# Counting out-degrees in the typed layer instead of beside the slot tables, and strewing GpSimd's marks among its fetches

## Chip, cores and metric

One core of one Trainium2 chip. The metric is the device time of one execution in microseconds (us), median of three runs. Shorter is better.

## What is computed

The reference is a graph network on 6250 nodes and 206250 edges (100000 random ones, the same turned round, and a self loop for each node, sorted by destination) with 128 features. Four layers follow each other, each added to its input and normalised:

```python
edge_index = jnp.stack([src, dst])
x = _layernorm(x + _L0_gnn_ref(x, ..., src, dst, edge_type_3, node_type_3), axis=-1)   # typed
x = _layernorm(x + _L1_gnn_ref(x, ..., edge_index, edge_weight), axis=-1)              # hyperbolic
x = _layernorm(x + _L2_gnn_ref(edge_index, x), axis=-1)                                # degree-normed
x = _layernorm(x + _L3_gnn_ref(x, edge_attr_64, src, dst, ...), axis=-1)               # edge features
```

Only the third layer needs the out-degree of every node, the number of edges with this source: `deg = segment_sum(ones, row)`, `norm = deg^-1/2[row] * deg^-1/2[col]`. The first, typed, layer sums a message of each edge, chosen by edge type and source type, into the edge's destination.

## The kernel before

All stages are blocks in which each engine runs its own queue; engines meet at semaphores, and at a barrier between blocks. The stages of this case, in order of time:

**Set-up (0 to 281 us).** Edges are loaded, their keys are made (`dbkt`, `dloc`: bucket of 128 nodes and place in it, of the destination; `sbkt`, `sloc`: the same of the source), and in-degrees are counted. The keys lie in `big`, the one large buffer, whose ranges are used again by the later stages. A count goes by batches of 16 columns (of 1612, so 101 batches): `hist_hot` makes on VectorE two one-hot tables in bf16, one of 128 places (L358, 128x2048) and one of 49 buckets (L359, 128x784), and `hist_sum` multiplies them on TensorE, 16 small matmuls (L366) into one PSUM tile. `hist_hot` of a batch waits for the matmuls of the batch two before it (`s_hist_mm`), since the tables are doubled.

**Slot tables (281 to 624 us, from L978).** 62 iterations (`GB`): 13 (`JB`) over slots that come from `chunk3`, a piece of the edge list loaded by four DMAs (L981, L982, `s_chunk`), and 49 (`NB`) over slots that GpSimd fetches, one indirect DMA of 128 x 4 KB for each (L1032, `s_took`, a ring of `GR` = 4). In iteration n VectorE and ScalarE pick keys (`pick`: L1087 to L1090, L1138, L1139), TensorE turns them (L1212), ScalarE stores them (L1145), VectorE splits the weight (L1099 to L1101) and SyncE writes the table out (L1001). In the same iterations the typed messages of a bucket of nodes are made: TensorE L1186, L1192, L1199, ScalarE L1150, L1156, L1163, L1164, SyncE's store L990. TensorE's `rows` (L1199) waits until ScalarE has emptied PSUM (L1164), and ScalarE's copy waits for TensorE.

GpSimd's queue in this stage is written out by hand: 49 indirect DMAs that put marks of 4 B into a table (L1016), one small gather (L1021), then the 49 fetches. Fetch b from the fifth on waits until slot table b + 9 has been picked. SyncE reads the marks back before table `MARK_LOAD` = 12 (L993), VectorE spreads them along the edges (`fill_forward`, before table `MARK_SCAN` = 20), and SyncE stores the result (L998, `edge_pairs`).

Out-degrees are counted here: `AHEAD` = 44 batches on VectorE and TensorE before the first pick, and the other 57 spread over the iterations (`outs(*shares[n])`), the last thing that an iteration does on TensorE.

**Adjacency blocks (624 to 2206 us)** use neither the keys nor the count.

**Typed layer (2206 to 3308 us, from L1558).** 456 groups of 512 edges. Of 24 groups (a turn) 13 come ready from DRAM by SyncE (L1564) and 11 are fetched by GpSimd, four indirect DMAs each (L1581, 836 in all), whose descriptors GpSimd prepares; I call that a preparation. SyncE brings their edge features (L1568). VectorE makes the one-hot table of a group (L1595, waits for TensorE's matmuls two groups back), adds the sums of the group two before it from PSUM to `acc` (L1620) and, in the first 17 turns, adds a step of the node's own row (L1612). TensorE does four matmuls a group (L1673) when table and features are there; PSUM banks 0 to 5 are a ring of Q = 6. A slot of the ring of QG = 8 fetched groups is free again when the matmuls eight groups back are done.

```python
pool.indirect_dma_start(out=got4[:, h, u, 0:D], out_offset=None, in_=typed_rows,
    in_offset=bass.IndirectOffsetOnAxis(ap=pairs4i[:, g, u, 0:1], axis=0)).then_inc(s_got[h], 16)
```

The pairs that this gather reads (`pairs4`) lie at the top of `big`. The functions that the change touches:

Of the kernel before, what the change touches and what calls it, by code (L numbers as in the profile page):

```python
# [147 lines left out]
def build(nc, x, src, dst, attr, etype, weight, ntype, w_e, b_e, w_n, b_n, w1, b1, w3, w3e, b3, out):  # L148
    ctx = ExitStack()
    with ctx:  # L150
# [90 lines left out]
        next_i = next_c.bitcast(I32)  # L241
        keys = []
        for _ in range(4):
            c, at = cut(at, CW // 2)
            keys.append(c.bitcast(BF16))
        dbkt, sbkt, dloc, sloc = keys
# [107 lines left out]
        def hist_hot(dve, lo, hi, n, c0, sl):  # L354
# [7 lines left out]
        def hist_sum(pe, to, n, sl, opens=False, closes=False):  # L362
# [405 lines left out]
        bias_sq = room(D)  # L768
        c1 = small[:, 11 * NB:11 * NB + 8]
# [200 lines left out]
        MARK_LOAD, MARK_SCAN = 12, 20  # L970
        AHEAD = 44
        shares = [(AHEAD + (HB - AHEAD) * n // GB, AHEAD + (HB - AHEAD) * (n + 1) // GB) for n in range(GB)]

        with nc.Block() as block:
# [36 lines left out]
            def _(pool):  # L1011
                pool.wait_ge(s_first, 1)
                beyond = pool.to_reg(MARKS - 1)
                for b in range(NB):
# [4 lines left out]
                pool.wait_ge(s_same, 1)  # L1019
                pool.sem_inc(s_turn, 1)  # L1020
                pool.indirect_dma_start(  # L1021
                    out=kind_i, out_offset=None, in_=ntype.rearrange("(n o) -> n o", o=1),
                    in_offset=bass.IndirectOffsetOnAxis(ap=head_i, axis=0)).then_inc(s_heads, 16)
                pool.iota(head_v, pattern=[[0, 1]], base=0, channel_multiplier=4 * CL,
                          allow_small_or_imprecise_dtypes=True).then_inc(s_pairs, 1)
                for b in range(NB):
                    n = JB + b
                    if b >= GR:
# [5 lines left out]
                        in_offset=bass.IndirectOffsetOnAxis(ap=first_i[:, b:b + 1], axis=0)).then_inc(s_took[b % GR], 16)  # L1034
                for k in range(GR):
# [3 lines left out]
            def _(dve):  # L1039
# [28 lines left out]
                def outs(j0, j1):  # L1068
                    for j in range(j0, j1):
                        hist_hot(dve, sloc, sbkt, HB + j, j * TT, (HB + j) % 2)  # L1070
                outs(0, AHEAD)
# [56 lines left out]
                dve.wait_ge(s_hist_mm, 2 * HB)  # L1128
                link(dve.tensor_copy(outdeg, out_count))
# [50 lines left out]
            def _(pe):  # L1180
                def outs(j0, j1):
                    for j in range(j0, j1):
                        hist_sum(pe, out_count, HB + j, (HB + j) % 2, opens=j == 0, closes=j == HB - 1)
# [19 lines left out]
                outs(0, AHEAD)  # L1203
                for n in range(GB):
# [13 lines left out]
                    outs(*shares[n])  # L1218
# [45 lines left out]
        pairs_at = big_words - NG * 2 * U  # L1264
        assert at <= pairs_at
        pairs4 = big[:, pairs_at:big_words].rearrange("p (g u r) -> p g u r", g=NG, u=U)
# [246 lines left out]
        xT4, at = cut(at, D)  # L1513
        assert at <= pairs_at
        OWN = 3
# [37 lines left out]
        with nc.Block() as block:  # L1553
# [33 lines left out]
            def _(dve):  # L1587
# [27 lines left out]
                def add(g, h, b, owned):  # L1615
# [22 lines left out]
                for r in range(LAG):  # L1638
                    add(NG - LAG + r, (NG - LAG + r) % Q, bucket[r], NB * OWN_STEPS)
# [12 lines left out]
            def _(pe):  # L1652
                pe.wait_ge(s_clear, 5)

                def turn(i, own_):
                    g0 = i * TURN
                    for pos in range(TURN):
                        h, k = pos % Q, pos % HS
# [11 lines left out]
                        slot_free(pe, s_acc, g0 + pos, Q)  # L1670
# [4 lines left out]
                        last.then_inc(s_mm, 1)  # L1675
                in_own_turns(pe, turn)
# [642 lines left out]
```

## Time and profile before

| | |
|---|---|
| median of 3 runs | 5259.34 us (5254.54 to 5260.63) |
| the profiled execution, its own time | 5261.47 us |
| its span, first to last instruction | 5259.7 us |
| mean granted TensorE clock | 0.934 |
| busy: PE, DVE, ACT, POOL | 72%, 62%, 23%, 43% |

PE is TensorE (PEld its weight loads), DVE VectorE, ACT ScalarE, POOL GpSimd, SP SyncE. A row of the timeline gives start and duration in us, engine, line, operation, output and input, and in brackets how long the engine had been idle and what ended that. "issue" is time in which an engine waited for nothing that the profile shows. The share of busy time is an average over stages with different limits, so each stage is read by itself.

### The profile page before, as it was taken

How to read it: one execution, taken by the hardware profiler on the slowest of the kernel's cores; microseconds unless marked ns; L12 is line 12 of the kernel's file. 1: busy time of each engine (PE TensorE's matmuls, PEld its weight loads, DVE VectorE, ACT ScalarE, POOL GpSimd, SP SyncE). 2: the span in 40 equal slices, each digit the busy share in tenths (PEclk: the TensorE clock that was granted, in tenths of full speed). 3: DMA queues.
4: the chain of work that ended last, by engine and by line, in shares of the span. 5: the costliest groups of instructions: out<-in, count | busy, mean ns of one | idle time of the engine just before them, and what ended most of it. 6: DMA issues, size and time to landing. Idle time of an engine off the chain costs nothing. (4 is left out here: it accounts for less than half of the span.)

```text
span 5259.7 us, 100150 instructions
## 1 busy us (share of the span) xinstructions
PE 3770.5 (72%) x38930; PEld 2751.6 (52%) x38930; DVE 3260.5 (62%) x4529; ACT 1204.4 (23%) x2110; POOL 2254.5 (43%) x2050
## 2 busy tenths in 40 slices
PE   4357755555555555377777676389999599989997
PEld 3345555555555555366666666345555244444444
DVE  7796898999999999455555554756666600230012
ACT  0025655555555555100000000400000200010000
POOL 0051378777777777577777777000000003000300
PEclk9998898999999999688998988699999799989998
DMA  9646797999999999865666656198888267656654
GB/s 315 212 115 238 236 343 276 327 346 340 336 338 340 343 344 330 222 165 166 171 165 165 169 162 158 22 332 305 301 305 304 91 203 227 198 165 202 217 187 142
DMA packets 695303, 1252.28 MB, mean 238 GB/s; under 512 B 366488, under 2 KB 511532, under 8 KB 685772
## 3 DMA queue, kind: packets, MB, share of 16 engines
q1 hardware_dynamic: 564028, 779.03, 46.1%
q10 hardware_dynamic: 60300, 314.88, 15.4%
q0 software_dynamic: 70576, 152.66, 11.4%
q8 instruction: 298, 4.88, 0.4%
q14 instruction: 101, 0.83, 0.0%
HBM read 792.49 MB, written 506.62 MB: 247 GB/s over the span
## 5 line engine op out<-in xcount | busy, mean ns | idle before, releaser
L1398 POOL DMA_INDIRECT big<-typed_msgs,big x988 | 1198.1, 1213 | 376.9 <-issue 307.8
L1446 PE MATMUL psum<-big 128*128 128x98 bf16 x7936 | 859.4, 208 | 649.8 <-DVE big L1428 629.4
L1446 PEld LDWEIGHTS psum<-big 128*128 128x128 bf16 x7936 | 766.0, 97 | 694.1 <-DVE big L1428 673.6
L2088 PE MATMUL psum<-big 128*128 128x512 bf16 (+1 forms) x4704 | 992.1, 373 | 82.6 <-DMA big<-adj 82.6
L1673 PE MATMUL psum<-big 128*128 128x192 f32 x3648 | 743.1, 364 | 307.8 <-DMA big<-typed_msgs,big 302.9
L1581 POOL DMA_INDIRECT big<-typed_msgs,big x836 | 830.8, 994 | 275.3 <-issue 244.8
L1673 PEld LDWEIGHTS psum<-big 128*128 128x128 f32 x3648 | 686.9, 215 | 371.8 <-issue 248.5
L1447 PE MATMUL psum<-big 128*128 128x49 bf16 x7936 | 845.5, 190 | 0.9 <-issue 0.9
L1448 PE MATMUL psum<-big 128*128 128x49 bf16 x7936 | 842.4, 186 | 2.7 <-issue 2.7
L1448 PEld LDWEIGHTS psum<-big 128*128 128x128 bf16 x7936 | 791.7, 100 | 3.1 <-issue 3.1
L2088 PEld LDWEIGHTS psum<-big 128*128 128x128 bf16 x4704 | 460.4, 98 | 605.9 <-DMA big<-adj 83.0
L1447 PEld LDWEIGHTS psum<-big 128*128 128x128 bf16 x7936 | 770.5, 97 | 11.1 <-issue 10.9
L1898 PE MATMUL psum<-big 128*128 128x416 f32 x1984 | 656.1, 494 | 63.4 <-DVE big L1932 62.4
L2135 POOL DMA_INDIRECT big<-spill,spill_row x98 | 92.7, 946 | 1420.0 <-DMA spill<-big 1390.7
L1428 DVE TENSOR_TENSOR big<-big 128x2400 bf16<-128x2400 bf16 x496 | 692.7, 1397 | 0.0
L1595 DVE SCALAR_TENSOR_TENSOR big<-iota,node,big 128x512 f32<-128x512 f32 x456 | 342.0, 750 | 517.4 <-PE psum L1673 502.5
L1425 DVE TENSOR_TENSOR big<-big 128x2048 bf16<-128x2048 bf16 x496 | 602.2, 1214 | 0.0
L1932 DVE STREAM_TRANSPOSE big<-big 128x3136 f32<-128x3136 f32 x124 | 427.2, 3445 | 239.6 <-PE psum L1898 221.2
L1486 ACT CAST big<-psum 128x784 bf16<-128x784 f32 x496 | 404.9, 816 | 675.7 <-PE psum L1448 574.7
L1898 PEld LDWEIGHTS psum<-big 128*128 128x128 f32 x1984 | 378.0, 191 | 341.1 <-issue 82.5
L1488 ACT COPY big<-psum 128x784 f32<-128x784 f32 x496 | 433.3, 874 | 0.0
L1423 DVE TENSOR_TENSOR big<-big 128x800 bf16<-128x800 bf16 x496 | 280.6, 566 | 68.9 <-POOLq L1402 50.1
(320 smaller groups left out, 2732.9 us busy)
## 6 DMA issues: line engine op xcount, KB each, us to landing
wadj<-big ACTq DMA_DIRECT2D x248, 784.0 KB
big<-wadj SPq DMA_DIRECT2D x124, 1568.0 KB, 7.3
big<-adj SPq DMA_DIRECT2D x210, 896.0 KB, 4.8
adj<-big ACTq DMA_DIRECT2D x62, 1568.0 KB
big<-staged SPq DMA_DIRECT2D x247, 384.0 KB, 3.3
staged<-big SPq DMA_DIRECT2D x61, 1536.0 KB
big<-edge_feats SPq DMA_DIRECT2D x456, 128.0 KB, 3.0
edge_feats<-in_edge_attr SPq DMA_DIRECT2D x1, 51562.5 KB, 163.3
```

Of the source, the lines that this page charges most:

```text
L1398: pool.indirect_dma_start(out=sgot4[:, c, u, 0:D], out_offset=None, in_=typed_rows, in_offset=bass.IndirectOffsetOnAxis(ap=pairs4i[:, g, u ...
L1425: dve.tensor_tensor(lo_b[:, q, :, :].rearrange("p t (c d) -> p t c d", d=2), in_twos(lo_ramp).to_broadcast([P, TT, P // 2, 2]), all_column ...
L1428: dve.tensor_tensor(hi_b[:, q, :, 1:4, :].rearrange("p t s (c d) -> p t s c d", d=2), hi.unsqueeze(2).to_broadcast([P, TT, 3, HC // 2, 2]) ...
L1446: pe.matmul(to[:, 0:2 * NB], lo, hi_b[:, q, t, 0:2, 0:NB], start=True, stop=False)
L1447: pe.matmul(to[:, NB:2 * NB], lo, hi_b[:, q, t, 2, 0:NB], start=False, stop=False)
L1448: last = pe.matmul(to[:, NB:2 * NB], lo, hi_b[:, q, t, 3, 0:NB], start=False, stop=True)
L1488: act.copy(wadj_st[:, k, b // 2, :, b % 2 * TT:(b % 2 + 1) * TT], made_in(b % 2)[:, :, NB:2 * NB].rearrange("p t s -> p s t")).then_inc(s_ ...
L1581: pool.indirect_dma_start(out=got4[:, h, u, 0:D], out_offset=None, in_=typed_rows, in_offset=bass.IndirectOffsetOnAxis(ap=pairs4i[:, g, u, ...
L1673: last = pe.matmul(ps[h][:, 0:ACCW], hot4[:, k, u, :], got4[:, pos % QG, u, :], start=(u == 0), stop=(u == U - 1))
L1898: last = pe.matmul(ps[c][:, 0:(b1 - b0) * 32], rows, turned[:, n % RT, q * QROW + b0 * 32:q * QROW + b1 * 32], start=(m == 0), stop=(m == ...
L1932: dve.transpose(turned[:, n % RT, :].rearrange("p (h i) -> p h i", i=32), wring[:, n % RW, :].rearrange("p (h g) -> p h g", g=32)).then_in ...
L2088: last = pe.matmul(ps[c % 2][:, 0:len(blocks) * P], terms_[:, k, b * D:(b + 1) * D], ring_a[:, m % RA, 0:len(blocks), s * P:(s + 1) * P], ...
```

## The change

The source keys `sbkt` and `sloc` move to the top of `big`, where they survive until the typed layer, and `pairs4` moves down below them. The 101 batches leave the slot tables; in the typed layer batch j is made on VectorE in group 4j + 1 and multiplied on TensorE after group 4j + 3, from tables of its own, and the count is copied out at the layer's end. Its PSUM tile lies in bank 5, so the ring of the group sums has 5 banks instead of 6. In GpSimd's queue the first four fetches come first, then the small gather, then three marks ahead of each further fetch; marks are read back before table 36 and spread before table 42.

```diff
-        MARK_LOAD, MARK_SCAN = 12, 20
-        AHEAD = 44
-        shares = [(AHEAD + (HB - AHEAD) * n // GB, AHEAD + (HB - AHEAD) * (n + 1) // GB) for n in range(GB)]
+        MARK_LOAD, MARK_SCAN = 36, 42
...
-                for b in range(NB):
+                def mark(b):
                     pool.sem_inc(s_turn, 1)
                     pool.indirect_dma_start(out=marks, ...).then_inc(s_marks, 16)
+                def fetch(b):
                     n = JB + b
                     if b >= GR:
                         pool.wait_ge(s_sb_st, n - GR + 1)
                         pool.wait_ge(s_slw_st, n - GR + 1)
                     ...
+                for b in range(GR):
+                    fetch(b)
+                pool.wait_ge(s_same, 1)
+                ...
+                marked_to = 0
+                for b in range(GR, NB):
+                    for m in range(marked_to, min(NB, marked_to + 3)):
+                        mark(m)
+                        marked_to = m + 1
+                    fetch(b)
...
-                outs(0, AHEAD)
                 dve.wait_ge(s_chunk, 16 * 4)
...
                         pick(n)
-                        outs(*shares[n])
...
-        pairs4 = big[:, pairs_at:big_words].rearrange("p (g u r) -> p g u r", g=NG, u=U)
+        pairs4 = big[:, pairs_at:kept_at].rearrange("p (g u r) -> p g u r", g=NG, u=U)
...
+        OUT_EVERY = NG // HB
+        PQ = 5
...
+                def out_hot(g):
+                    j, r = divmod(g, OUT_EVERY)
+                    if r == 1 and j < HB:
+                        hist_hot(dve, sloc, sbkt, HB + j, j * TT, (HB + j) % 2, out_lo, out_hi)
...
                         one_hot(i, pos)
                         ...
-                            add(g0 + (pos - LAG), (pos - LAG) % Q, bucket[pos % Q], owned)
+                            add(g0 + (pos - LAG), bucket[pos % Q], owned)
+                        out_hot(g0 + pos)
                         own(i, pos, own_)
...
+                dve.wait_ge(s_hist_mm, 2 * HB)
+                dve.tensor_copy(outdeg, out_count).then_inc(s_clear, 1)
+                dve.wait_ge(s_clear, 6)
...
-                        slot_free(pe, s_acc, g0 + pos, Q)
+                        slot_free(pe, s_acc, g0 + pos, PQ)
...
                         last.then_inc(s_mm, 1)
+                        c, r = divmod(g0 + pos, OUT_EVERY)
+                        if r == 3 and c < HB:
+                            hist_sum(pe, out_count, HB + c, (HB + c) % 2, opens=c == 0, closes=c == HB - 1, lo_hot=out_lo, hi_hot=out_hi)
```

GpSimd's queue in the slot tables before the change; 206336x1 is the table of marks, 128x1024 a fetch, 128x1 the small gather:

```order
L1016 DMA marks<-big 206336x1 x49
L1021 DMA big<-in_node_type,big 128x1
L1024 IOTA big 128x1
L1032 DMA big<-edge_fields,big 128x1024 x49
```

The same queue after it, down to the third group of marks (line numbers are those of the changed kernel: L1019 marks, L1029 fetches):

```order
L1029 DMA big<-edge_fields,big 128x1024 x4
L1036 DMA big<-in_node_type,big 128x1
L1039 IOTA big 128x1
L1019 DMA marks<-big 206336x1 x3
L1029 DMA big<-edge_fields,big 128x1024
L1019 DMA marks<-big 206336x1 x3
L1029 DMA big<-edge_fields,big 128x1024
L1019 DMA marks<-big 206336x1 x3
```

The groups of three go on through 16 fetches, and a 49th mark stands before the 17th; 29 more fetches follow with nothing between them.

VectorE's queue in the typed layer after the change, where a batch falls (L1601 is the one-hot table of a group, L1632 the add, L362 and L363 the two tables of the batch, L1618 the step of the node's own row):

```order
L1601 SCALAR_TENSOR_TENSOR big<-iota,node,big 128x512
L1632 ISA
L1632 TENSOR_TENSOR big<-psum,big 128x192
L362 TENSOR_TENSOR big<-ramp,big 128x2048
L363 TENSOR_TENSOR big<-ramp,big 128x784
L1618 SCALAR_TENSOR_TENSOR big<-bnb,nmask,big 128x128
L1601 SCALAR_TENSOR_TENSOR big<-iota,node,big 128x512
```

Before, the same rows stood there without L362 and L363: the batch is new between the add and the own step of every fourth group.

## Rows read from the trace of the kernel before

**Rows 1.** Busy time by stretch: us, PE, PEld, DVE, ACT, POOL busy, PEclk, DMA share, GB/s
```profile
404.00:609.50 205.50, 163.06 (x1282) 123.32 (x1280) 143.99 (x310) 129.12 (x362) 42.88 (x45) 0.88 0.79 273
2206.00:3292.00 1086.00, 769.08 (x3739) 705.39 (x3739) 561.62 (x1196) 27.89 (x97) 830.79 (x836) 0.89 0.61 165
```

**Rows 2.** The page's costliest groups: busy, mean ns, idle before and its releaser
```profile
L1581 POOL DMA_INDIRECT big<-typed_msgs,big x836 | 830.8, 994 | 275.3 <-issue 244.8
```

**Rows 3.** Waits from 2206 to 3310 us: total us, times, longest
```profile
POOL big L1581 <- issue: 244.8, 803, 0.3
PE psum L1673 <- DMA big<-typed_msgs,big: 302.9, 146, 4.8
```

**Rows 4.** Timeline of the slot tables up to the fifth fetch
```profile
318.86 0.42 ACT L1138 COPY big<-big 128x128 f32<-128x128 f32 x1 [74.15 <-DMA big<-edge_fields]
...
355.44 1.31 POOL L1016 DMA_INDIRECT marks<-big  x1 [0.30 <-issue]
355.82 0.56 DVE L359 TENSOR_TENSOR big<-ramp,big 128x784 bf16<-128x784 bf16 x1
...
404.14 0.94 POOL L1032 DMA_INDIRECT big<-edge_fields,big  x1 [34.47 <-ACT big L1139]
```

**Rows 5.** Timeline of the slot tables, one round between TensorE and ScalarE
```profile
375.28 0.80 ACT L1164 COPY big<-psum 128x768 f32<-128x768 f32 x1
...
376.23 2.17 PE L1199 MATMUL psum<-wnT,big 128*128 128x384 f32 x6 [1.03 <-ACT big L1164]
...
378.44 0.48 ACT L1163 COPY big<-psum 128x384 f32<-128x384 f32 x1
```

**Rows 6.** Timeline of the slot tables: one stall, fetches of later iterations, the end
```profile
492.43 0.48 ACT L1145 CAST big<-psum 128x384 bf16<-128x384 f32 x1 [18.89 <-DMA slot_tabs<-big]
...
544.29 0.94 POOL L1032 DMA_INDIRECT big<-edge_fields,big  x1 [2.90 <-ACT big L1139]
547.83 0.94 POOL L1032 DMA_INDIRECT big<-edge_fields,big  x1 [2.60 <-ACT big L1139]
...
609.42 1.14 POOL L1032 DMA_INDIRECT big<-edge_fields,big  x1 [1.92 <-DVE big L1090]
...
622.59 0.48 ACT L1145 CAST big<-psum 128x384 bf16<-128x384 f32 x1 [3.11 <-DMA slot_tabs<-big]
```

**Rows 7.** DMA from 520 to 580 us; a fetch's median us to landing
```profile
DMA packets 6680, 19.82 MB, mean 330 GB/s; under 512 B 737, under 2 KB 2718, under 8 KB 6674
...
big<-edge_fields,big POOLq DMA_INDIRECT x16, 6.5
```

**Rows 8.** Timeline of the slot tables: GpSimd beside a batch of the count
```profile
360.59 0.97 POOL L1016 DMA_INDIRECT marks<-big  x1 [0.30 <-issue]
...
361.37 1.21 DVE L358 TENSOR_TENSOR big<-ramp,big 128x2048 bf16<-128x2048 bf16 x1
...
364.52 1.22 DVE L358 TENSOR_TENSOR big<-ramp,big 128x2048 bf16<-128x2048 bf16 x1
...
365.04 1.52 POOL L1032 DMA_INDIRECT big<-edge_fields,big  x1 [0.30 <-issue]
...
365.65 0.56 DVE L359 TENSOR_TENSOR big<-ramp,big 128x784 bf16<-128x784 bf16 x1
```

**Rows 9.** Timeline of the typed layer: a delayed preparation, two places where batches will stand
```profile
2235.56 0.35 DVE L1620 TENSOR_TENSOR big<-psum,big 128x192 f32 x1
2236.04 0.95 POOL L1581 DMA_INDIRECT big<-typed_msgs,big  x1 [0.30 <-issue]
...
3166.84 0.35 DVE L1620 TENSOR_TENSOR big<-psum,big 128x192 f32 x1
...
3167.34 0.94 POOL L1581 DMA_INDIRECT big<-typed_msgs,big  x1 [0.30 <-issue]
...
3259.78 0.75 DVE L1595 SCALAR_TENSOR_TENSOR big<-iota,node,big 128x512 f32<-128x512 f32 x1 [3.19 <-PE psum L1673]
3259.94 1.41 POOL L1581 DMA_INDIRECT big<-typed_msgs,big  x1 [0.30 <-issue]
```

More of the change, by code:

```diff
@@ L241, in build @@
         next_i = next_c.bitcast(I32)
+        kept_at = big_words - CW
+        kept_keys = big[:, kept_at:big_words].bitcast(BF16)
         keys = []
-        for _ in range(4):
+        for _ in range(2):
             c, at = cut(at, CW // 2)
             keys.append(c.bitcast(BF16))
-        dbkt, sbkt, dloc, sloc = keys
+        dbkt, dloc = keys
+        sbkt, sloc = kept_keys[:, 0:CW], kept_keys[:, CW:2 * CW]
+        keys += [sbkt, sloc]
         masks_at = at
@@ L768, in build @@
         bias_sq = room(D)
+        assert r_at[0] <= kept_at
         c1 = small[:, 11 * NB:11 * NB + 8]
@@ L1018, in _ @@
                         in_=mark_v[:, b:b + 1], in_offset=None, bounds_check=beyond, oob_is_err=False).then_inc(s_marks, 16)
[L1019 to L1026, printed above, removed]
+                def fetch(b):
                     n = JB + b
@@ L1034, in _ @@
                         in_offset=bass.IndirectOffsetOnAxis(ap=first_i[:, b:b + 1], axis=0)).then_inc(s_took[b % GR], 16)
+                for b in range(GR):
+                    fetch(b)
+                pool.wait_ge(s_same, 1)
+                pool.sem_inc(s_turn, 1)
+                pool.indirect_dma_start(
+                    out=kind_i, out_offset=None, in_=ntype.rearrange("(n o) -> n o", o=1),
+                    in_offset=bass.IndirectOffsetOnAxis(ap=head_i, axis=0)).then_inc(s_heads, 16)
+                pool.iota(head_v, pattern=[[0, 1]], base=0, channel_multiplier=4 * CL,
+                          allow_small_or_imprecise_dtypes=True).then_inc(s_pairs, 1)
+                marked_to = 0
[4 more added lines that the diff above has]
+                    fetch(b)
                 for k in range(GR):
@@ L1066, in _ @@
                 link(dve.tensor_scalar(spill_row[:, :], row_f, none, None, ALU.add))
-                def outs(j0, j1):
-                    for j in range(j0, j1):
-                        hist_hot(dve, sloc, sbkt, HB + j, j * TT, (HB + j) % 2)
-                outs(0, AHEAD)
                 dve.wait_ge(s_chunk, 16 * 4)
@@ L1180, in _ @@
             def _(pe):
-                def outs(j0, j1):
-                    for j in range(j0, j1):
-                        hist_sum(pe, out_count, HB + j, (HB + j) % 2, opens=j == 0, closes=j == HB - 1)
                 def turn(b):
@@ L1201, in rows @@
                     made.then_inc(s_z, 1)
-                outs(0, AHEAD)
                 for n in range(GB):
@@ L1217, in _ @@
                         rows(n - 2)
-                    outs(*shares[n])
         typed_rows = typed_msgs.rearrange("n (t f) -> (n t) f", t=KINDS)
@@ L1513, in build @@
         xT4, at = cut(at, D)
+        out_lo, at = cut(at, 2 * P * TT // 2)
+        out_hi, at = cut(at, 2 * NB * TT // 2)
+        out_lo = out_lo.bitcast(BF16).rearrange("p (k g c t) -> p k g c t", k=2, g=TG, t=TU)
+        out_hi = out_hi.bitcast(BF16).rearrange("p (k g c t) -> p k g c t", k=2, g=TG, t=TU)
         assert at <= pairs_at
+        OUT_EVERY = NG // HB
+        PQ = 5
         OWN = 3
@@ L1613, in own, with add @@
                                              ALU.mult, ALU.add).then_inc(s_own, 1)
-                def add(g, h, b, owned):
+                def out_hot(g):
+                    j, r = divmod(g, OUT_EVERY)
+                    if r == 1 and j < HB:
+                        hist_hot(dve, sloc, sbkt, HB + j, j * TT, (HB + j) % 2, out_lo, out_hi)
+                def add(g, b, owned):
+                    h = g % PQ
                     dve.wait_ge(s_mm, g + 1)
@@ L1638, in _ @@
                 for r in range(LAG):
-                    add(NG - LAG + r, (NG - LAG + r) % Q, bucket[r], NB * OWN_STEPS)
+                    add(NG - LAG + r, bucket[r], NB * OWN_STEPS)
+                dve.wait_ge(s_hist_mm, 2 * HB)
+                dve.tensor_copy(outdeg, out_count).then_inc(s_clear, 1)
+                dve.wait_ge(s_clear, 6)
             @block.scalar
@@ L1657, in turn @@
                     for pos in range(TURN):
-                        h, k = pos % Q, pos % HS
+                        h, k = (g0 + pos) % PQ, pos % HS
                         j, r = divmod(pos, OWN_EVERY)
```

8 lines of the change are left out of this document (3 added, 5 removed).

## The prediction

> **What bounds the kernel now.** I read the busy time by stretch first, since the page's shares are means over stages. Two stages hold what changes. In the typed layer no engine but one is close to its limit by its duty: GpSimd's 836 preparations fill 830.8 of 1086 us [rows 1, 2]. What counts is its idle time: the table of waits puts 244.8 us on "issue", 803 times 0.3 us [rows 3]. So between two preparations there is a fixed gap of 0.30 us and nothing else; 836 x (0.994 + 0.30) = 1082 us is the whole stretch. TensorE waits 302.9 us for just these fetches [rows 3]. The typed layer is GpSimd's: TensorE and VectorE have room there, but every us added to a preparation is added to the stage.
>
> In the slot tables the chunk of edges is there at 318.86, when ScalarE's first copy starts, but VectorE goes on counting to 355.82 + 0.56 = 356.4 and, three small instructions later, picks at 356.8 [rows 4]. That is the first thing to be had. Later an iteration takes 3.84 us (idle 2.90 and 0.94 between two fetches) and one that has no batch 3.54 [rows 6]. The reason is one round between TensorE and ScalarE [rows 5]: ScalarE's copy ends at 376.08, TensorE's L1199 runs from 376.23 to 378.40, ScalarE copies again from 378.44 for 1.2 us. This is 3.55 us without any batch; the batch makes TensorE's own sum 3.84. From 520 to 580 us the DMA engines move 330 GB/s [rows 7], 1.27 MB an iteration (messages 576 KB, fetch 512, table 160), so DMA is near its bound too.
>
> **The changed parts, slot tables.** One thing at a time, from the first pick on.
>
> *Start.* The 44 early batches go; the first pick waits for the chunk. Four fetches, 2.1 MB, are now issued beside that load; at 330 GB/s they take 6.4 us. Pick 0 moves from 356.8 to between 319 (fetches cost nothing) and 328 (they go at 234 GB/s, the 7 MB of the load over some 30 us); I take 326. Gain 31 us, bounds 29 to 38.
>
> *Iterations 0 to 13.* From 356.8 to the fifth fetch's start at 404.14 [rows 4] it is 47.3 us, with batches. At 3.55 us less the short first ones I take 45. Gain 2.5 us. Pick 13 is then done at 371.
>
> *Marks among fetches.* Only the first three marks use the time in which GpSimd is idle (34.47 us [rows 4]). The fifth fetch waits for pick 13, and 46 marks and 16 more fetches stand behind it. Free of VectorE one takes 0.94 to 0.97 and the gap 0.30 [rows 4, 8], so four are 5.1 us, 5.2 with small hold-ups, against 3.55 to 3.7 for an iteration. The ring of four gives about 14 us, less the 6.5 to landing [rows 7]; after some five iterations GpSimd leads. The 17th such fetch starts at 371 + 16 x 5.2 = 454 and pick 33 follows at about 460; at 3.7 us from pick 13 it would be at 445, and in the kernel before the 20 iterations took 77 us without stalls. So this part loses 12.5 us (bounds: 0, if marks cost no time beside the fetches, and 20).
>
> *The rest.* Iterations up to 51 can't get much below 3.7 us, since 1.27 MB at 345 GB/s are that: 18 x 0.13 = 2 us. The last eleven take 1.92 + 1.14 = 3.06 us with a batch [rows 6]; without it the wait for the table's store stays (3.11 us of idle at 622.59 [rows 6]), and I take 2.4: gain 7 us (0 to 15). The stalls behind the marks' load and the store of pairs (18.89 us the longest [rows 6]) only move to tables 36 and 45; I cost this at nothing, with 8 us either way.
>
> Sum for the slot tables: 31 + 2.5 - 12.5 + 2 + 7 = **30 us gained**, bounds 18 to 45.
>
> **The changed parts, typed layer.** 101 batches arrive. TensorE gets 101 x 0.95 us (16 matmuls) = 96 us; it lies inside the 302.9 us in which TensorE waits for fetches [rows 3], and the fetch ring of eight groups covers a late group. VectorE gets 101 x 1.7 = 170 us on 562 of 1086 [rows 1], covered likewise. If this cover were gone, a group would come up to 1.7 us late. The fifth PSUM bank isn't missed, the add is two groups behind. SyncE's queue gets nothing. The copy at the end costs 0.5 us.
>
> What isn't covered is GpSimd. One preparation starts 0.52 us after L358 (365.04 against 364.52) [rows 8]. It ends at 366.56, 2.04 us after L358's start, and takes 1.52 instead of 0.95. It got through 0.35 us after L359's start (365.65) and needed 0.56 from there. The same holds for two-operand work in f32: the preparation of 3259.94, started under L1595, took 1.41 [rows 9]. So a preparation that starts u after L358 loses 1.09 - u. One that is under way when L358 starts loses nothing: that of 360.59 took 0.97 [rows 8]. GpSimd starts one every 1.25 us. With u anywhere between 0 and 1.25 the mean loss is 1.09 x 1.09 / 2 / 1.25 = 0.48 us, with the little that L359 adds 0.56, or 57 us over 101 batches. But VectorE follows GpSimd's fetches, so u isn't free. I laid a batch behind the add of each group 4j + 1 in this trace: at the third place it would start at 2235.83 and meet the preparation of 2236.04, losing 0.88; at the last, 3167.11 against 3167.34, losing 0.86 [rows 9]. Of the 101 places 43 are like these, 41 lose some 0.16, the others nearly nothing, in sum 46 us, 0.46 each. I take **46 us lost**; the bounds are 5 (all in the kind phase) and 110 (all in the worst).
>
> The Trainium skill (SBUF — State Buffer, section "SBUF: two separate sides") says that VectorE and GpSimd share a port pair as "an **exclusive lock**, not a bandwidth split", which whoever starts first has for its whole instruction. By that rule a preparation under way would hold VectorE up as well; L358 at 361.37, begun inside the preparation of 360.59, took its usual 1.21 [rows 8], so this trace doesn't agree in that half.
>
> **Sum.** 5261.5 (the profiled execution's own time) - 30 + 46 + 0.5 = 5278; that execution lay 2 us above the median of the runs, so 5276 on the median's scale. I say 5275. About 0.2%, 10.5 us, can be told from no change; this is 0.3% slower.
>
> **Rivals.**
> *No change to be seen.* Hold-ups at 0.2 to 0.4 each (a delayed preparation shifts the next, which may draw the phase to the kind side, where 41 places lie already) make 20 to 40 us, as much as the gain: 5250 to 5270, say 5261. For it: the two sums are alike, and each is uncertain by 10 and 20.
> *Faster.* If GpSimd's preparations settle in step with VectorE, so that each starts just before a batch, the loss is 0.1 each, 10 us, and with 30 to 35 gained the time is 5237. For it: the marks before the change ran in such a step, 1.31 + 0.30 = 1.61 us each with 44 batches of 1.61, losing 0.36 [rows 4]; against it: here three groups pass between two batches. It decides at a mean below 0.19 us.
> *The hold-up spans VectorE's whole run.* One-hot, add and batch stand back to back, 2.6 us. If a preparation gets no chance between them it waits for the run's end: 0.68 a batch from the batch alone (69 us, 5298), up to 1.25 with the one-hot (126 us, 5355). Against it: L358 to L359 let one through [rows 8]. The exclusive lock of the Trainium skill's page, read strictly over a chain of such instructions, would give this.
> *The marks are not hidden as the change says.* That is in my sum; if GpSimd were fast enough after all, 12 us more are gained, which moves the forecast to 5263.
>
> **Chances.** Slower as forecast or more 0.42 (of it 0.06 for the whole-run case), no change 0.32, faster 0.26. The likeliest case's own range is 5270 to 5298. The range for 8 in 10 reaches to the other two: low 5236, the faster rival; high 5305, the loss of 75 us.
>
> **What would show it.** ScalarE's and VectorE's first picks both at about 326. Fetches between picks 18 and 33 every 5.2 us, with marks back to back and GpSimd idle only 0.30 between. The slot tables end near 594 instead of 624. In the typed layer POOL's gap stays at 0.30, the mean of its 836 preparations rises from 994 to about 1050 ns, and its delayed ones lie at L362. I am wrong if that mean stays below 1015 ns, if GpSimd's waits there end on TensorE (then the ring, not the port, is short), or if the first pick stays beyond 335.

## The result, and the profile after

| | before | changed |
|---|---|---|
| median | 5260.63 us (5254.54 to 5265.01, 5 runs) | 5282.14 us (5277.71 to 5294.26, 5 runs) |
| ratio | | 1.0047 [1.0031, 1.0062] |
| profiled execution: own time, span | 5261.47, 5259.7 | 5277.71, 5276.0 |
| pick 0, 13, 33, 51 (VectorE's L1090, now L1098) | 357.20, 401.09, 518.37, 587.87 | 325.17, 365.33, 455.05, 561.12 |
| last split begins (L1101, now L1109) | 623.97 | 591.66 |
| adjacency: first preparation (L1398) | 634.31 | 602.15 |
| typed layer: first and last preparation (L1581, now L1587) | 2206.25, 3290.69 | 2176.35, 3312.63 |

The change makes the kernel 0.4 to 0.5% slower: 21.5 us between the medians, some 25 by the ratio. The profiled execution was the quickest of the five, so its span shows only 16.3 us of that. The slot tables end 32.2 us earlier (first preparation of the adjacency blocks), the adjacency blocks take 2.3 us more, and the typed layer takes 1136.3 us from its first to its last preparation instead of 1084.4: 51.9 us given back where 32 had been gained. What follows the typed layer was 5.6 us shorter; its code is the same, and its length differs by up to 7 us between the profiles of the fast chip.

The start of the slot tables, from the timeline of the changed kernel:

```profile
286.93 0.93 POOL L1029 DMA_INDIRECT big<-edge_fields,big  x1 [0.30 <-issue]
...
324.19 0.42 ACT L1143 COPY big<-big 128x128 f32<-128x128 f32 x1 [79.83 <-DMA big<-edge_fields]
...
325.17 0.38 DVE L1098 SCALAR_TENSOR_TENSOR big<-big 128x128 f32<-128x128 f32 x1
...
368.09 1.01 POOL L1029 DMA_INDIRECT big<-edge_fields,big  x1 [37.35 <-ACT big L1144]
...
372.00 0.97 POOL L1019 DMA_INDIRECT marks<-big  x1 [0.30 <-issue]
372.40 0.39 DVE L1098 SCALAR_TENSOR_TENSOR big<-big 128x128 f32<-128x128 f32 x1
373.28 0.98 POOL L1029 DMA_INDIRECT big<-edge_fields,big  x1 [0.30 <-issue]
...
378.43 0.98 POOL L1029 DMA_INDIRECT big<-edge_fields,big  x1 [0.30 <-issue]
```

Against [rows 4]: ScalarE's first copy comes 5.3 us later than before (the four fetches are now issued beside the chunk's load; with the old order back, in the run marks first, it comes at 319.22), but VectorE picks 0.98 us after it and no longer 38 us after it. From the fifth fetch on, while marks are left, GpSimd is idle for 0.30 or 0.31 us between any two of its DMAs, and a fetch with its three marks takes 5.14 to 5.33 us.

The typed layer: first the stretch (us, then busy time of PE, PEld, DVE, ACT, POOL, the granted clock, the DMA share and GB/s), then the row of the preparations on the page, then the waits from 2176 to 3332 us (total us, times, longest).

```profile
2176.00:3313.00 1137.00, 843.16 (x5355) 773.64 (x5355) 709.03 (x1398) 27.90 (x97) 882.13 (x836) 0.90 0.59 158
```

```profile
L1587 POOL DMA_INDIRECT big<-typed_msgs,big x836 | 882.7, 1056 | 273.8 <-issue 248.4
```

```profile
PE psum L1689 <- DMA big<-typed_msgs,big: 272.4, 141, 5.0
POOL big L1587 <- issue: 248.4, 815, 0.3
```

Against [rows 1 to 3]: the gap between two preparations is still 0.30 us, TensorE still waits for the fetches, and the mean preparation went from 994 to 1056 ns. 882.7 - 830.8 = 51.9 us is the whole growth of the stage. TensorE (+74 us busy) and VectorE (+147 us) took the batches into their idle time: TensorE's waits for these fetches fell from 302.9 to 272.4 us.

One place in the timeline, the kind of which the 51.9 us are made:

```profile
3028.18 1.21 DVE L362 TENSOR_TENSOR big<-ramp,big 128x2048 bf16<-128x2048 bf16 x1
3028.19 2.02 POOL L1587 DMA_INDIRECT big<-typed_msgs,big  x1 [0.30 <-issue]
3029.31 0.56 DVE L363 TENSOR_TENSOR big<-ramp,big 128x784 bf16<-128x784 bf16 x1
```

A preparation that starts 0.01 us after the batch's first table should, by the rule of the prediction, lose 1.09 - 0.01 us; it took 2.02 instead of 0.95. The rule has the length right, and the moment can be told more simply than the prediction did. A preparation counts as held up here when it took over 0.97 us. All 356 of them began under a VectorE instruction, and all ended 0.81 to 0.83 us after the end of just that instruction. "0.35 us after the start of VectorE's next instruction, and 0.56 more" gives the same time only because the next instruction mostly starts 0.08 us before the first one's end. Where nothing follows, the end still decides; a place in the kernel before:

```profile
2825.03 0.35 DVE L1612 SCALAR_TENSOR_TENSOR big<-bnb,nmask,big 128x128 f32<-128x128 f32 x1
2825.18 1.03 POOL L1581 DMA_INDIRECT big<-typed_msgs,big  x1 [0.30 <-issue]
...
2828.02 0.75 DVE L1595 SCALAR_TENSOR_TENSOR big<-iota,node,big 128x512 f32<-128x512 f32 x1 [2.64 <-PE psum L1673]
```

The preparation ends at 2826.21, 0.83 us after the step's end at 2825.38, though VectorE starts nothing before 2828.02. So a preparation that begins under such an instruction waits for that instruction's end, and the split of its time into 0.35 and 0.56 us is nothing that the traces show.

### The profile page after: what moved, and what is told of

The parts are those of the page before. It is cut to its first block and busy times, and to the rows that moved or that the text cites. A ratio compares the mean times of both kernels' runs of the same rounds, so it can differ in the third digit from the quotient of the medians.

```text
span 5276.0 us, 100150 instructions
## 1 busy us (share of the span) xinstructions
PE 3762.8 (71%) x38930; PEld 2735.1 (52%) x38930; DVE 3246.1 (62%) x4529; ACT 1201.8 (23%) x2110; POOL 2287.4 (43%) x2050
## 3 DMA queue, kind: packets, MB, share of 16 engines
q10 hardware_dynamic: 60300, 314.88, 15.4%
## 5 line engine op out<-in xcount | busy, mean ns | idle before, releaser
L1398 POOL DMA_INDIRECT big<-typed_msgs,big x988 | 1196.0, 1210 | 379.2 <-issue 309.7
L1587 POOL DMA_INDIRECT big<-typed_msgs,big x836 | 882.7, 1056 | 273.8 <-issue 248.4
L1689 PE MATMUL psum<-big 128*128 128x192 f32 x3648 | 746.5, 362 | 282.8 <-DMA big<-typed_msgs,big 272.4
L1689 PEld LDWEIGHTS psum<-big 128*128 128x128 f32 x3648 | 674.7, 212 | 345.7 <-issue 224.0
L1601 DVE SCALAR_TENSOR_TENSOR big<-iota,node,big 128x512 f32<-128x512 f32 x456 | 341.4, 749 | 426.3 <-PE psum L1689 408.3
L1917 PEld LDWEIGHTS psum<-big 128*128 128x128 f32 x1984 | 377.7, 190 | 340.7 <-issue 81.9
```

Source lines behind the costliest of these rows:

```text
L1398: pool.indirect_dma_start(out=sgot4[:, c, u, 0:D], out_offset=None, in_=typed_rows, in_offset=bass.IndirectOffsetOnAxis(ap=pairs4i[:, g, u ...
L1689: last = pe.matmul(ps[h][:, 0:ACCW], hot4[:, k, u, :], got4[:, pos % QG, u, :], start=(u == 0), stop=(u == U - 1))
L1917: last = pe.matmul(ps[c][:, 0:(b1 - b0) * 32], rows, turned[:, n % RT, q * QROW + b0 * 32:q * QROW + b1 * 32], start=(m == 0), stop=(m == ...
```

## The experiments

Each set of kernels ran on one chip, beside the kernel before. There were four sets, and the kernel before took 5873.5 us in the first and 5818.6 in the third, but 5257.6 and 5261.0 in the second and fourth. I call the first and third "slow chips" and the other two "the fast chip". That it is the chip itself and not what ran beside the core is not shown (the last section says more). On the slow chips the typed layer isn't GpSimd's. Most of those kernels ran again on the fast chip, and from the slow chips I read the length of the preparations and not the total.

**No batches at all.** The calls of `out_hot` and of `hist_sum` in the typed layer are dropped:

```diff
-                        out_hot(g0 + pos)
...
-                        if r == 3 and c < HB:
-                            hist_sum(pe, out_count, ...)
...
-                dve.tensor_copy(outdeg, out_count).then_inc(s_clear, 1)
+                dve.memset(outdeg, 33.0).then_inc(s_clear, 1)
```

> The changed kernel without the 101 batches of the out-degree count in the typed layer: neither VectorE's two tables nor TensorE's 16 matmuls each; the degree is set to 33, so the third layer's norm isn't the reference's. Theory A (GpSimd's preparations are held up by VectorE's table pairs, the typed layer is GpSimd's): the mean of the 836 preparations falls from 1056 to about 994 ns, the stage is 50 us shorter, the time about 5232, 27 to 30 us under the kernel before (ratio 0.9945). Theory B (the loss lies elsewhere, as in the ring of five banks or the moved pairs): the time stays above 5260.

> Part left out: the out-degrees are not counted at all; all of them are set to 33. So only the 30 us of the slot tables remain of the change. My theory (the batches lengthen GpSimd's preparations, and each us is added to the typed layer): mean preparation back at about 994 ns, the layer 50 us shorter than in the changed kernel, 5232 us, ratio 0.9945 to before. Rival (the typed layer grew for another reason, the ring of 5 PSUM banks or the moved table of pairs, which this kernel keeps): it stays near 5282, ratio 1.004. On the slow kind of chip 0.995 to 1.000 by either.

On the slow chip: 5872.47 us, ratio 0.9995 [0.9982, 1.0008], mean preparation 974 ns. On the fast one: 5225.57 us, 0.9942 [0.9928, 0.9955]. The row of the preparations there, from the table of groups, and two waits from 2180 to 3260 us:

```profile
L1587 POOL DMA_INDIRECT big<-typed_msgs,big x836 | 821.2, 982 | 275.1 <-issue 246.9 <-POOLq L1356 20.6 <-PE psum L1687 7.6
```

```profile
PE psum L1687 <- DMA big<-typed_msgs,big: 307.1, 154, 5.4
POOL big L1587 <- issue: 246.9, 810, 0.3
```

With the ring of five PSUM banks and the moved keys still in place the layer is short again; so neither of them costs anything that shows, and the batches cost all of it: 882.7 - 821.2 = 61.5 us against this run, 0.61 each; against the kernel before, whose own preparations averaged 994 ns, 0.51 each. The traces tell these two apart. If what each preparation took above 0.945 us is put to the instruction under which it began, 50.9 us fall to the tables of the batches (47.9 under L362, 3.0 under L363), and 55.3 in the profile of the changed kernel run again: 0.50 to 0.55 a batch. The one-hot tables of the groups have the rest: 42.0 and 37.8 us in the two profiles of the changed kernel, 39.2 in the kernel before and 30.9 in the run without batches. So the 10 us between 0.51 and 0.61 are hold-ups under the one-hots, and those differ between executions even without a batch: the kernel before with 22 batches ahead (below) has the same typed layer as the kernel before, and 27.5 us of them.

**The changed kernel again**, as the control of the second set.

> The changed kernel once more, unaltered, as the control for the others of this set. The first set of runs came from a chip on which the kernel before took 5873 us instead of 5261, with waits in the typed layer that ended outside the trace. If this chip is like the first one: ratio 1.0047 to the kernel before, some 5282 us, mean preparation 1056 ns. If it is the slow kind: a ratio between 0.995 and 1.000, since there TensorE's and VectorE's waits in the typed layer, not GpSimd's preparations, set its length, while the 30 us of the slot tables stay.

5285.33 us (5279.94 to 5287.62), ratio 1.005 [1.0036, 1.0064], mean 1056 ns again; typed layer from 2178.73 to 3315.00, 1136.3 us. Its span is 23.9 us above the one before: 29.8 gained up to the adjacency blocks, 2.3 lost in them, 51.9 lost in the typed layer.

**What of a batch holds GpSimd up.** Once only the two tables are made, with no matmul behind them. Once VectorE is busy for as long and the matmuls stay, but it only writes:

```diff
-                        hist_hot(dve, sloc, sbkt, HB + j, j * TT, (HB + j) % 2, out_lo, out_hi)
+                        dve.memset(out_lo_f[...1024 words], 0.0)
+                        dve.memset(more[...640 words], 0.0)
+                        dve.memset(out_hi_f[...392 words], 0.0).then_inc(s_hist_hot, 1)
```

> The changed kernel with VectorE's table pairs but without TensorE's matmuls on them (the degree is set to 33). Theory A: TensorE's 96 us lie in its waits for fetches, so this takes what the changed kernel takes, within 5 us: about 5280, mean preparation 1050 to 1060 ns. Rival C (TensorE's extra matmuls delay the groups): the time falls towards 5232 and the mean preparation stays at 1056 while GpSimd's waits shrink.

> The changed kernel with each table pair replaced by three memsets (1024, 640 and 392 words, by the length of the memset of 9408 words in 7.90 us some 0.86 + 0.54 + 0.33 us = 1.73 less the overlap), followed by the same matmuls; the count is zero and the degree is set to 33. VectorE is as busy as with the pairs, but reads nothing. Theory A in the form that the hold-up comes from VectorE reading two operands from SBUF: preparations beside the memsets stay at 0.95 us, mean near 994 ns, time 5230 to 5237. Rival D (any VectorE work of 1.7 us holds a preparation up, or the delay of VectorE's own chain is what costs): mean near 1050 ns, time near 5280.

> Parts left out: the one-hot tables of the out-degree batches; in their place VectorE writes zeros of the same length in three memsets, the matmuls stay, the degrees are all set to 33. Theory (a preparation is held up by VectorE instructions that read two operands from SBUF, not by VectorE being busy): mean preparation 975 to 995 ns instead of 1056, typed layer 45 to 60 us shorter than the changed kernel's 1136, in all 5225 to 5240 us, ratio 0.994 to 0.997. Rival (any long VectorE instruction holds GpSimd up, or the added matmuls and the later groups cost the time): mean 1030 ns or more, 5265 or more, ratio above 1.001. This chip may be of the slow kind, where the time tells nothing; then the mean of the preparations decides.

All three fell on slow chips: 5856.31 us, 0.997 [0.9955, 0.9985]; 5887.17, 1.0023 [1.001, 1.0037]; 5833.13, 1.003 [1.0019, 1.0042]. The totals don't follow the batches there: with the tables the kernel took 16 us less than without them (5872.47), with the memsets 15 more, and the reason stays open. So the times that were expected of these runs are not tested. The rows of the preparations can be compared all the same; from the pages of the run without batches, with the tables alone, and of the two with memsets, in this order:

```profile
L1587 POOL DMA_INDIRECT big<-typed_msgs,big x836 | 813.9, 974 | 521.9 <-issue 240.3
```

```profile
L1587 POOL DMA_INDIRECT big<-typed_msgs,big x836 | 862.6, 1032 | 454.3 <-issue 240.5
```

```profile
L1589 POOL DMA_INDIRECT big<-typed_msgs,big x836 | 804.0, 962 | 543.3 <-issue 223.9
```

```profile
L1589 POOL DMA_INDIRECT big<-typed_msgs,big x836 | 814.2, 974 | 512.4 <-issue 228.0
```

Two tables of 1.21 and 0.56 us add 48.7 us to the preparations, with no matmul in sight. Three memsets of 0.91, 0.59 and 0.39 us, with all the matmuls, add nothing (962 and 974 ns against 974). In the timeline of the second run with memsets:

```profile
2628.73 0.91 DVE L1628 MEMSET big<- 128x1024 f32 x1 [0.16 <-issue]
2629.49 0.95 POOL L1589 DMA_INDIRECT big<-typed_msgs,big  x1 [0.30 <-issue]
2629.72 0.59 DVE L1629 MEMSET big<- 128x640 f32 x1
```

A preparation that starts in the middle of a memset takes its usual 0.95; over 200 began under the two longer memsets in the two runs, and none took more than 0.96. So it is not that VectorE is busy, but what it does: the tables read two operands from SBUF, the memsets none. Whether one operand would be enough can be read from the kernel before, since the add of a group (L1620) reads one operand from PSUM and one from SBUF:

```profile
2237.19 0.35 DVE L1620 TENSOR_TENSOR big<-psum,big 128x192 f32 x1
2237.29 0.95 POOL L1581 DMA_INDIRECT big<-typed_msgs,big  x1 [0.30 <-issue]
```

Of 122 preparations that began under this add none took more than 0.96 us. Of the 239 under the one-hot (L1595), which reads two operands from SBUF, 203 were held up. The step of the node's own row (L1612) settles it, for it is one line with two forms: with its first operand in PSUM it held none of 40, with both in SBUF 14 of 28.

The Trainium skill (SBUF — State Buffer, section "SBUF: two separate sides") names just this class, a VectorE operation with two SBUF inputs against a GpSimd operation that reads SBUF, and gives the first to start the ports for its whole instruction. The runs agree with it where VectorE is first: the preparation ends 0.81 to 0.83 us after the end of the instruction under which it began, and it gets through there although the next one, L363 behind L362, reads two operands as well. There are exceptions: in the run with other groups (below) 12 preparations that began under L362 waited for the end of L363 too, the longest 2.49 us, and why is open.

**GpSimd's old order in the changed kernel.** All marks, the gather, then all fetches; marks read back before table 12.

```diff
-        MARK_LOAD, MARK_SCAN = 36, 42
+        MARK_LOAD, MARK_SCAN = 12, 20
...
-                for b in range(GR):
-                    fetch(b)
+                for b in range(NB):
+                    mark(b)
...
-                for b in range(GR, NB):
-                    for m in range(marked_to, min(NB, marked_to + 3)):
-                        mark(m)
-                        marked_to = m + 1
-                    fetch(b)
+                for b in range(NB):
+                    fetch(b)
```

> The changed kernel with GpSimd's old order in the slot tables: 49 marks, the gather, then the fetches, and marks read before table 12 and spread before table 20. Theory E (strewing the marks costs time, since four issues of 1.29 us a fetch are longer than an iteration): the chunk lands at 319 instead of 324, the marks are done by 347 in time in which GpSimd idled, the fifth fetch starts at pick 13 near 363, and iterations 13 to 33 go at 3.6 instead of 5.2 us where GpSimd leads. The slot tables end 15 to 20 us earlier, the time is 5262 to 5267. Rival F (DMA bounds those iterations anyway, or the stall of the marks' load grows when it falls early): gain under 6 us.

> The changed kernel with GpSimd's old order: all 49 marks, the small gather, then the 49 fetches, marks read back before table 12 and spread before table 20. Theory A (the fetches between picks 18 and 33 go at 5.2 us because of the marks among them, and that costs 12 to 15 us; the 49 marks ahead, 61 us from 283, end at 345, and the first fetched table is wanted only after pick 13 at about 371): slot tables shorter by 10 to 18 us than in the changed kernel, 5264 to 5272 us, ratio 1.001 to 1.002. Theory B (the strewing hides the marks as the change says): the marks ahead delay the fetches and with them the stage, same time or up to 15 us longer, 5282 to 5297, ratio 1.004 to 1.007.

Slow chip: 5864.71 us, 0.9978 [0.9966, 0.9989]. Fast chip: 5270.44 us, 1.0026 [1.0016, 1.0036], 15 us less than the changed kernel of the same set. Two fetches one behind the other in its timeline:

```profile
466.59 0.94 POOL L1029 DMA_INDIRECT big<-edge_fields,big  x1 [2.60 <-ACT big L1140]
470.13 0.94 POOL L1029 DMA_INDIRECT big<-edge_fields,big  x1 [2.60 <-ACT big L1140]
```

GpSimd has its 2.60 us of idle time back, an iteration takes 3.54 us, and the first preparation of the adjacency blocks comes at 588.78 instead of 604.53. The strewing, with the marks read back at table 36 instead of 12, costs 15 us; the marks ahead are done by 348, before the fifth fetch is wanted. (From the kernel before this one differs by 45.5 us in this stage: 37.0 up to the first pick, and 8.5 that I put to the 57 batches beside the tables, 0.15 each.)

**Part of the count in each place.** Marks first; 22 batches while VectorE waits for the chunk, one in each of the first 49 tables, 30 in the typed layer:

```diff
+        AHEAD, BESIDE = 22, 22 + 49
...
+                outs(0, AHEAD)
                 dve.wait_ge(s_chunk, 16 * 4)
...
+                    if n < NB:
+                        outs(AHEAD + n, AHEAD + n + 1)
...
+                    j += BESIDE
...
-                dve.tensor_copy(outdeg, out_count).then_inc(s_clear, 1)
+                dve.tensor_tensor(outdeg, out_count, outdeg, ALU.add).then_inc(s_clear, 1)
```

> A third way to place the count: marks first as before, 22 batches while VectorE and TensorE wait for the chunk of edges, one in each of the first 49 tables, and only the last 30 in the typed layer. Theory (the 22 lie in the wait before the chunk and cost nothing, a batch in a table iteration costs 0.3 us where TensorE sets the round but the iterations with nothing better to do hide it, a batch in the typed layer costs 0.5): slot tables 35 to 43 us shorter than before, typed layer 15 longer, some 5236 us, ratio 0.9945 to 0.997, faster than both kernels. Rival (the cost of a batch in the tables is as large as in the typed layer): 5255 to 5262, ratio 0.999 to 1.000.

5238.04 us (5230.57 to 5241.71), ratio 0.996 [0.9946, 0.9974]: faster than both kernels, as expected. The typed layer takes 1094.4 us with a mean preparation of 1006 ns, and a table with one batch takes 3.84 us:

```profile
480.31 0.94 POOL L1030 DMA_INDIRECT big<-edge_fields,big  x1 [2.92 <-ACT big L1149]
484.15 0.94 POOL L1030 DMA_INDIRECT big<-edge_fields,big  x1 [2.91 <-ACT big L1149]
```

**One number of the kernel before.** If a batch beside a table costs 0.15 us and one in the typed layer 0.5, none should be in the typed layer:

```diff
-        AHEAD = 44
+        AHEAD = 22
```

> The kernel before with one number changed: 22 batches ahead of the first pick instead of 44, the other 79 spread over the 62 tables; no batch in the typed layer, marks first. Theory (the wait behind the chunk was the whole fault of the old placing; a batch beside a table costs 0.14 to 0.16 us, since the slot tables of the run with the marks first and no batch at all were 45.5 us shorter than before, of which 37.6 are the start, 7.9 the 57 batches): start 36 to 38 us earlier, 22 more batches beside the tables 3 to 7 us, in all 29 to 35 us faster than before, 5224 to 5232 us, ratio 0.993 to 0.9945, level with or just better than the split count. Rival (with 79 batches in 62 tables VectorE or TensorE becomes the bound there, 0.5 us and more for each of the added): 5240 or more, ratio above 0.996.

> The kernel before with 22 batches ahead of the first pick instead of 44, once more, since its first run fell on a chip of the slow kind (the kernel before 5819 us there, this one 1.0029 of it, with ScalarE stopped for 18.6 us at a table store among the marks). On a chip like the first (the kernel before near 5258 us): as expected of it there, 5224 to 5232 us, ratio 0.993 to 0.9945, by the theory that the wait behind the chunk was the whole fault of the old placing and a batch beside a table costs 0.14 to 0.16 us. Rival (79 batches in 62 tables make VectorE or TensorE the bound, or the first tables run into the marks' read back as on the slow chip): 5240 or more, ratio above 0.996. On a slow chip: 1.002 to 1.004 again.

Slow chip: 5833.45 us, 1.0029 [1.0017, 1.0041]; ScalarE stood there for 18.64 us while the marks ran, until something that the core's own trace doesn't show ("remote"):

```profile
359.79 0.48 ACT L1145 CAST big<-psum 128x384 bf16<-128x384 f32 x1 [18.64 <-remote]
```

Fast chip: 5250.75 us (5241.54 to 5265.69), ratio 0.9982 [0.9973, 0.9991], faster than before but not by the 30 us expected. My theory fell. The rival's time came true; its cause, an engine that becomes the bound, has to be read from the trace. The first pick is at 322.12, but of its 35 us only 9 are left at the first preparation of the adjacency blocks (625.32). With 79 batches in 62 tables 17 tables have two, and there (timeline on the fast chip):

```profile
482.66 0.94 POOL L1032 DMA_INDIRECT big<-edge_fields,big  x1 [2.91 <-ACT big L1139]
483.70 0.95 PE L366 MATMUL psum<-big 128*128 128x49 bf16 x16
...
484.68 1.23 DVE L358 TENSOR_TENSOR big<-ramp,big 128x2048 bf16<-128x2048 bf16 x1 [2.14 <-PE psum L366]
...
487.46 0.40 DVE L1090 SCALAR_TENSOR_TENSOR big<-big 128x128 f32<-128x128 f32 x1
487.55 1.74 PE L366 MATMUL psum<-big 128*128 128x49 bf16 x32
...
488.67 1.91 POOL L1032 DMA_INDIRECT big<-edge_fields,big  x1 [5.07 <-DVE big L1090]
```

The second table pair of an iteration waits for the matmuls of the batch two before it, and TensorE multiplies batches only at the end of an iteration. So VectorE stands still for 2.14 us, the split and the next pick (L1090) come behind that, and the time to the next fetch is 6.01 us (482.66 to 488.67) instead of 3.84. Seventeen times 2.17 are 37 us; 26 us came through, 1.5 for each such table, since the picks after it often follow at 3.06 us until the loss is partly made good. So what costs is the wait of the second pair, and not that either engine has too much to do. One batch in a table costs some 0.15 us, a second one 1.5. That fits that the split count, one in each of 49 tables, is the better one (0.996 against 0.9982, in two sets), although it pays for 30 in the typed layer.

**Other groups for the batches.** Laid by my rule on the trace without batches, some groups of a turn lose less than others:

```diff
-        OUT_EVERY = NG // HB
+        OUT_AT = (2, 3, 7, 10, 11, 15)
...
-                    if r == 1 and j < HB:
+                    j = i * len(OUT_AT) + (OUT_AT.index(r) if r in OUT_AT else HB)
+                    if j < HB:
```

> The changed kernel with each batch in another group: behind the adds of groups 2, 3, 7, 10, 11 and 15 of each turn of 24 instead of 1, 5, 9, 13, 17, 21. Laid on the trace without batches by my rule (a preparation that starts u after the batch's first table loses 1.09 - u) these six places lose 0.28, 0.31, 0.33, 0.24, 0.20 and 0.38 on average, together some 30 us for 101 batches, the places of the changed kernel 0.45, 0.48, 0.66, 0.60, 0.51 and 0.72. If the phase is fixed by the place in the turn: 15 to 25 us less than the changed kernel, 5260 to 5270 us, ratio 1.000 to 1.002. Rival (each held-up preparation shifts the next ones, so that after a few batches the phase is as good as random wherever they stand): mean stays near 1056 ns and the time within 8 us of the changed kernel, ratio 1.003 to 1.006.

Slow chip: 5830.59 us, 1.0022 [1.0013, 1.0032], mean 1011 ns. The nearest run with the old places on a slow chip, the one with the marks first, has 1018. That is 6 us over 836 preparations and two different sets: it tells nothing, and whether a better place would save 20 us on a fast chip stays open.

## Why the prediction was right

It said 5275 us, 0.3% slower, by 30 us gained in the slot tables and 46.5 lost in the typed layer. Measured were 5282, slower by 0.5%. The mechanism held: GpSimd's preparations carry the loss, and they are held up by the tables. Point by point, from the profiled executions:

- *Start*: first pick forecast at 326, was at 325.17; 32.0 us gained for 31.
- *Iterations 0 to 13*: 2.5 us forecast, 43.9 - 40.2 = 3.7 measured.
- *Marks among fetches*: forecast 12.5 us lost between picks 13 and 33. Before, these took 117.3 us, of which 42.5 are three stalls (iterations of 15.4, 15.0 and 22.6 us, less 3.5 each), 74.8 without them; after, 89.7 with none: 14.9 lost. The run with the marks first gives 15 for the same thing. The place was a little off: the picks follow each other at some 3.5 us up to pick 21 (394.03) and at 5.1 on average only from there, where I had said 18.
- *The rest to pick 51*: 2 us forecast. 69.5 us before; after, 106.1 less stalls of 12.1, 12.1 and 19.2 makes 62.7: 6.8 gained. Part of that gain is what GpSimd had fetched ahead during the stalls: two picks follow at 1.45 and 1.60 us behind the second one. The stalls moved and grew by 0.9 in sum, costed at nothing. The two waits of 12 us and more now stand at tables 40 and 42, the long one at table 49; I had said 36 and 45.
- *Tail*: 7 us forecast, 32.8 - 27.8 = 5.0 measured from pick 51 to pick 61.
- *Typed layer*: 46 us forecast, 51.9 measured. Of a batch's loss I forecast 43 large, 41 small and 17 near nothing; 48, 33 and 20 came (above 0.6 us, 0.12 to 0.6, below). The losses laid on the old trace held although the added batches shift everything behind them. The gap stayed at 0.30, the mean came to 1056 ns for "about 1050", and the waits didn't move to TensorE.

The term that was too small is the typed layer's, 51.9 measured for 46. The losses laid under L362 were nearly right, 47.9 us. What was missing is 3.0 us under L363, which the laid sum left out, and 2.8 us more under the one-hots, against some 2 us less elsewhere. The range I gave for the term, 5 to 110, was far wider than needed. What the prediction has wrong is the moment at which a preparation gets through: it depends on the end of the instruction that holds it and not on the start of the next, which gives the same 1.09 - u for a batch.

That the sum comes so near is luck in part. For the profiled execution it said 5278, and 5277.7 came. But the gain in the slot tables was 32.2 for 30 (its terms were off by -2.4, +4.8 and -2.0, which nearly cancel), the loss 51.9 for 46.5, and two terms it didn't have, +2.3 in the adjacency blocks and -5.6 behind the typed layer, made up for that. The run again, in which the last term is absent (its rest is as long as before), came to 5285.

Of the rivals, *no change to be seen* is out: 0.50 to 0.55 a batch instead of 0.2 to 0.4, and the phase was not drawn to the kind side (20 places near nothing for 17, but 48 large ones for 43). *Preparations locked in step* is out: 48 of 101 places lost over 0.6 us. *The hold-up spans VectorE's whole run* is out by the row at 3028.19: the preparation ended 0.82 us after L362 had ended, while L363, an own step (L1618, 3029.79) and a one-hot table (L1601, 3030.05) followed without a gap. So a preparation gets through between two instructions of such a chain. *If GpSimd were fast enough* didn't come true: with the marks first 15 us are gained, so they are not hidden among the fetches.

## What to carry to other kernels

Before work is moved into the idle time of an engine, look at what it does to the engine that is the bound there: a VectorE instruction with two SBUF operands costs VectorE nothing in such a stage, but an indirect DMA of GpSimd that begins under it ends 0.82 us after its end; here that was half a microsecond a batch. An early stall (here 38 us of counting behind data that had landed) is cured by doing as much of the work ahead as fits the wait, and spreading the rest thinly enough that no iteration holds two pieces of it. Measure both halves of a change apart: this one was a gain of 32 us and a loss of 52, and neither needed the other.

## What of the hardware was not expected

The same kernel was 11 to 12% slower in two sets of four: 5873.5 and 5818.6 us against 5257.6 to 5261.0. The record gives the chips of the sets, in order, the numbers 0, 0, 5 and 12, so a slow set and a fast one bear the same number. Whether they are two chips or one at two times it doesn't say. A preparation takes its 0.94 to 0.97 us there too, and VectorE's L362 its 1.22. But the stages are longer (no batches: adjacency blocks 1878.5 us, typed layer 1295.8, against 1576.2 and some 1075 on the fast chip), and the waits end on something that the core's own trace doesn't show, "remote". From 2500 to 3810 us of the run without batches on the slow chip:

```profile
DVE big L1601 <- remote: 423.9, 117, 7.1
POOL big L1587 <- issue: 240.3, 732, 2.5
POOL big L1587 <- remote: 139.8, 62, 3.9
```

In the adjacency blocks DMA moved 276 GB/s there and 332 on the fast chip, at a granted clock of 0.78 instead of 0.97 (700 to 2100 us, from two windows):

```profile
700.00:2100.00 1400.00, 866.24 (x18052) 794.27 (x18050) 1122.77 (x1130) 642.26 (x848) 976.47 (x754) 0.78 0.80 276
```

```profile
700.00:2100.00 1400.00, 811.91 (x21954) 761.19 (x21950) 1349.04 (x1375) 789.94 (x1026) 1096.54 (x901) 0.97 0.96 332
```

The first is the run with the tables only, the second the changed kernel run again. What makes the slow sets slow stays open: the chip, or other work on it at the time. But there GpSimd is not the bound of the typed layer: its waits on "remote" come on top of its own gaps, and the kernel without any batch took as long as the kernel before (0.9995), where it gained 0.6% on the fast chip. A verdict on a change of half a per cent holds for the conditions in which it was measured.
